# Attention layer on one core: contexts stored unfinished, a third transpose bank, and the mask penalty split between GpSimd and TensorE

## The reference

```python
scale, shift = split(silu(sin_emb(timestep)) @ W_ada + b_ada)
x = ln(src) * (1 + scale) + shift
q, k, v = heads(x @ Wq + bq), heads(x @ Wk + bk), heads(x @ Wv + bv)
scores = q / sqrt(32) @ k.T + attention_bias          # bias: (2, 16, 2048, 2048), 512 MB
scores = where(src_mask, -inf, scores)                # mask: (2, 1, 2048, 2048)
ctx = softmax(scores) @ v
x = x + ctx @ Wo + bo
x = x + gelu2(ln(x) * g2 + beta2) @ W1 ... @ W2 + b2  # gelu2(z) = z * sigmoid(1.702 z)
out = rotate pairs of x by theta and phi
```

## Time and profile before

| | us |
|---|---|
| median of the runs shown | 3857.47 |
| the profiled execution | 3858.61 |
| its span, first to last instruction | 3857.0 |
| phase B, first add to last add and its step | 2172.4 |
| start of phase C, up to its first up-projection | 55.0 |
| the rest of phase C | 1080.6 |

### The profile page before, as it was taken

How to read it: one execution, slowest core, us unless ns; L and a number is a source line. 1 busy time by engine, 2 the same in 40 slices (tenths; PEclk the granted TensorE clock), 3 DMA queues, 4 the chain that set the end, 5 groups by cost and what they waited for, 6 DMA issues and landing times. The chain is left out here.

```text
span 3857.0 us, 64984 instructions
## 1 busy us (share of the span) xinstructions
PE 3589.8 (93%) x18848; PEld 2074.9 (54%) x18848; DVE 2561.2 (66%) x4882; ACT 1899.6 (49%) x2483; POOL 2165.7 (56%) x595
## 2 busy tenths in 40 slices
PE   6778769999999999999999999999699999999997
PEld 2334336666666666666666666666344444444443
DVE  3444449999989999899999899999322323232232
ACT  1221227777777777777777777777211111111110
POOL 0000059999989999999999999999000000000000
PEclk8889879999999999999999999999799999999999
DMA  5556489999999999999999999997511101101000
GB/s 188 169 173 201 147 288 319 315 313 312 319 348 317 316 312 312 337 331 313 317 315 313 341 319 314 317 313 271 155 22 33 22 11 33 22 22 22 11 11 11
DMA packets 327444, 822.20 MB, mean 213 GB/s; under 512 B 165376, under 2 KB 181760, under 8 KB 250624
## 3 DMA queue, kind: packets, MB, share of 16 engines
q1 hardware_dynamic: 277376, 746.44, 57.6%
q10 hardware_dynamic: 45312, 58.74, 5.6%
q0 software_dynamic: 4736, 16.78, 1.2%
HBM read 737.95 MB, written 83.89 MB: 213 GB/s over the span
## 5 line engine op out<-in xcount | busy, mean ns | idle before, releaser
L450 POOL TENSOR_TENSOR ring<-ring,penb 128x2048 f32<-128x2048 f32 x512 | 2089.4, 4119 | 599.6 <-DMA penb<-pen_scratch 542.5
L555 ACT ACTIVATE ring<-ring,neg_max 128x2048 f32<-128x2048 f32 x512 | 1029.1, 2010 | 515.4 <-DVE neg_max L520 515.4
L618 PEld LDWEIGHTS b_T<-ident,ring 128*128 128x128 f32 x8192 | 886.7, 141 | 623.5 <-ACT probT L564 427.6
L618 PE MATMUL b_T<-ident,ring 128*128 128x128 f32 x8192 | 1158.7, 281 | 1.9 <-DVE probT L492 1.3
L492 DVE COPY probT<-b_T 128x512 f32<-128x512 f32 x1024 | 668.0, 684 | 70.5 <-PE b_T L618 70.5
L506 DVE CUSTOM_DVE_ANT_0 ring<-scores,ring,max_part 128x1024 f32<-128x1024 f32 x512 | 657.6, 1284 | 74.2
L506 DVE CUSTOM_DVE_ANT_0 ring<-scores,ring 128x1024 f32<-128x1024 f32 x512 | 622.2, 1215 | 43.6 <-PE scores L601 43.6
L601 PE MATMUL scores<-keys,queries 128*128 (+1 forms) x2048 | 606.5, 418 | 46.6 <-DMA queries<-q_parts 45.4
L781 POOL TENSOR_TENSOR y_out<-rot_a,rot_b 128x512 f32<-128x512 f32 x32 | 50.3, 1572 | 1020.8 <-DVE rot_b L890 1020.0
L564 ACT COPY probT<-b_T 128x512 f32<-128x512 f32 x1024 | 542.8, 580 | 30.2 <-PE b_T L618 24.0
L634 PE MATMUL bank_ctx<-probT,values 128*32 128x512 f32 x4096 | 546.8, 607 | 0.0
(11 more groups left out here) (91 smaller groups left out, 1926.1 us busy)
## 6 DMA issues: line engine op xcount, KB each, us to landing
ring<-in_fside_Bx16xSxS SPq DMA_DIRECT2D x512, 1024.0 KB, 5.8
keys<-k_parts SPq DMA_DIRECT2D x256, 256.0 KB, 6.8
values<-v_heads ACTq DMA_DIRECT2D x128, 256.0 KB, 6.0
queries<-q_parts SPq DMA_DIRECT2D x512, 64.0 KB, 6.8
pen_scratch<-pen SPq DMA_DIRECT2D x8, 2048.0 KB, 7.2
penb<-pen_scratch SPq DMA_DIRECT2D x32, 512.0 KB, 12.3
xin<-in_x ACTq DMA_DIRECT2D x8, 1024.0 KB, 5.2
mask_in<-in_mask_Bx1xSxS_bk ACTq DMA_DIRECT2D x8, 1024.0 KB, 7.3
```

The source lines that it names most:

```text
L450: nc.gpsimd.tensor_tensor(ring[:, j, :], ring[:, j, :], penb[:, j, :], ALU.add).then_inc(masked, 1)
L555: nc.scalar.activation(ring[:, k, :], ring[:, k, :], ACT.Exp, bias=neg_max[:, k:k + 1], accum_out=sums[:, k:k + 1]).then_inc(exp_done, 1)
L618: last = nc.tensor.transpose(bankT[n % 2][:, c * P:(c + 1) * P], ring[:, slot, at:at + P], ident[:])
```

## The change

Phase B:
- GpSimd adds the penalty to columns 0 to 1855 only. For the last 192 columns TensorE adds it, with one more matmul per tile: identity (bf16) times `penb`, accumulated on top of the second half's scores.
- The adds produce the negated sum (`scale=-1`) and its minimum, so that the exponential takes its bias from them directly; `neg_max` is gone. The 8 row minima of a trip are kept in `low_all` by a VectorE copy of 128 x 8 (`keep_low`), once per trip, after the first add of the next trip. The row sums go straight into `sums_all`.
- `close`, the reciprocal and the context product are gone from phase B. `ctxp`, the four partial contexts, is stored as it is: 256 KB instead of 64 KB per unit.
- The bank of `bank_sum` becomes a third transpose bank. Even tiles turn their quarters into banks 0, 1, 2, 0, odd ones into 2, 1, 0, 2.
- VectorE copies quarter 3 of tile i-3 between the two adds of tile i, and quarter 2 of tile i-2 after them.
- TensorE's waits are moved ahead into the group of matmuls before the one that needs them.

Phase C: TensorE transposes reciprocals, widened by VectorE to 128 columns (`recip_wide`), instead of contexts. VectorE adds the four parts (`tensor_reduce`) and multiplies; ScalarE's copy is gone. Contexts are loaded as 4 MB per unit in 16 transfers instead of 1 MB in 4.

The core of the diff:

```diff
-                        nc.gpsimd.tensor_tensor(ring[:, j, :], ring[:, j, :], penb[:, j, :], ALU.add).then_inc(masked, 1)
+                        nc.gpsimd.tensor_tensor(ring[:, j, 0:POOL_MASKED], ring[:, j, 0:POOL_MASKED], penb[:, j, 0:POOL_MASKED], ALU.add).then_inc(masked, 1)
...
+        def turn_bank(t, n):
+            return bankT[(0, 1, 2, 0)[n] if t % 2 == 0 else (2, 1, 0, 2)[n]]
...
-            def copy_quarter(it, j, n):
-                t, k = it * R + j - 2, (j - 2) % R
+            def copy_quarter(it, j, n, lag):
+                t, k = it * R + j - lag, (j - lag) % R
...
+            def keep_low(it, j):
+                if j == 0 and (not known(it) or it > 0):
+                    dve.wait_ge(added, it * R * CH)
+                    nc.vector.tensor_copy(low_all[:, bass.ds(it - 1, 1), :].rearrange("p o n -> p (o n)"), low[:]).then_inc(low_kept, 1)
...
             def step(it, j):
                 add(it, j, 0)
+                keep_low(it, j)
+                copy_quarter(it, j, 3, 3)
                 add(it, j, 1)
-                if live(i, NT):
-                    dve.wait_ge(added, i * CH + CH)
-                    nc.vector.tensor_scalar(neg_max[:, j:j + 1], max_part[:, j, CH - 1:CH], -2.0, 0.5, ALU.mult, ALU.mult).then_inc(max_ready, 1)
-                copy_quarter(it, j, 2)
...
-                copy_quarter(it, j, 3)
...
+                copy_quarter(it, j, 2, 2)
...
             # TensorE, inside score(it, j, c)
+                for n in range(CW // N):
+                    if n == CW // N - 1:
+                        free_before_turn(it, j, c)   # c 0: exp_done t + 1; c 1: out_dve t * 2 - 1
...
+                    if c == CH - 1:
+                        pe.wait_ge(pen_in[j], (it // H) * 16 + 16)
+                        last = nc.tensor.matmul(scores[c][:, CW - PE_MASKED:CW], identb[:], penb[:, j, POOL_MASKED:S],
+                                                start=False, stop=True)
...
             def turn(it, j, n):
                 t, slot = it * R + j - 2, (j - 2) % R
+                for c in range(QR):
+                    if c == 2:
+                        if n == 0 and live(t, NT):
+                            need(pe, out_act, t * 2)
+                        if n == 1:
+                            copied_before_weigh(it, j)
+                        if n == 2 and live(t, NT):
+                            pe.wait_ge(out_act, t * 2 + 1)
...
             def weigh(it, j):
+                for c in range(4):
+                    if c == 2 and live(t, NT):
+                        need(pe, out_dve, t * 2)
+                    if live(unit, UNITS):
                         last = nc.tensor.matmul(bank_ctx[DH * c:DH * (c + 1), :], values[:, hh, QR * n + c, :],
                                                 probT[:, hh, QR * n + c, :], start=(n == 0), stop=(n == 3))
...
-                if j % QT == 2:
-                    close(it, j)
...
             # phase C, VectorE, front(v, f)
                 if f == 0:
+                    nc.vector.tensor_scalar(undefined[:], in_unit(low_all, v), 2.0, 0.0, ALU.mult, ALU.mult)
+                    link(nc.vector.reciprocal(recip[:], in_unit(sums_all, v)), 1)
+                    link(nc.vector.tensor_tensor(recip[:], recip[:], undefined[:], ALU.add), 2)
+                    need(dve, wo_done, v * QT)
+                if f < DB:
+                    need(dve, recip_turned, v * DB + f - 1)
+                    nc.vector.tensor_copy(recip_wide[:, f % 2].rearrange("p t (h d) -> p t h d", d=DH),
+                                          recip[:, 4 * f:4 * f + 4, :].rearrange("p h (t o) -> p t h o", o=1).to_broadcast([P, QT, 4, DH])).then_inc(wide_ready, 1)
+                    dve.wait_ge(part_ld[f % 2], v * 128 + (f // 2) * 64 + 64)
+                    nc.vector.tensor_reduce(ctxT[:, f, :], parts[:, f % 2].rearrange("p g q -> p q g"), AXIS_X, ALU.add).then_inc(parts_used, 1)
+                    dve.wait_ge(parts_used, v * DB + f + 1)
+                    dve.wait_ge(recip_turned, v * DB + f + 1)
+                    nc.vector.tensor_tensor(ctxT[:, f, :], fore[f % 2][:], ctxT[:, f, :], ALU.mult).then_inc(ctxT_ready, 1)
+                if f == 3:
                     dve.wait_ge(xm_ld, v * 16 + 16)
...
             # phase C, TensorE, front(v, f)
                 if f < DB:
-                    if f == 0:
-                        pe.wait_ge(ctx_ld, v * 64 + 64)
+                    pe.wait_ge(wide_ready, v * DB + f + 1)
...
-                        last = nc.tensor.transpose(fore[f % 2][:, t * P:(t + 1) * P], ctx_in[:, t, 4 * f:4 * f + 4, :].rearrange("p h d -> p (h d)"), ident[:])
+                        last = nc.tensor.transpose(fore[f % 2][:, t * P:(t + 1) * P], recip_wide[:, f % 2, t, :], ident[:])
```

More of the change, by code:

```diff
@@ L606, in turn, with free_before_turn @@
+            def free_before_turn(it, j, c):
+                t = it * R + j - 2
+                if live(t, NT):
+                    if c == 0:
+                        pe.wait_ge(exp_done, t + 1)
+                    else:
+                        need(pe, out_dve, t * 2 - 1)
             def turn(it, j, n):
                 t, slot = it * R + j - 2, (j - 2) % R
-                if live(t, NT):
-                    if n == 0:
-                        pe.wait_ge(exp_done, t + 1)
-                    if n < 2:
-                        need(pe, out_dve, t * 2 - 1 + n)
-                    else:
-                        pe.wait_ge(out_act, t * 2 - 1 + n)
-                    for c in range(QR):
-                        at = (QR * n + c) * P
-                        last = nc.tensor.transpose(bankT[n % 2][:, c * P:(c + 1) * P], ring[:, slot, at:at + P], ident[:])
-                    last.then_inc(turned, 1)
@@ L621, in weigh @@
-            def weigh(it, j):
-                n = (j - 2) % QT
-                unit = it * 2 - 2 if j < 2 else it * 2 - 1 if j < 6 else it * 2
-                hh = 1 if 2 <= j < 6 else 0
-                if live(unit, UNITS):
-                    if n == 0:
-                        pe.wait_ge(v_in[hh], it * 16 if j == 2 else it * 16 + 16)
-                        need(pe, ctx_copied, unit)
-                    pe.wait_ge(out_act if n < 2 else out_dve, (unit * QT + QT - 1) * 2 + n % 2 + 1)
-                    for c in range(4):
+                for c in range(QR):
[6 more added lines that the diff above has]
+                            pe.wait_ge(out_act, t * 2 + 1)
+                    if live(t, NT):
+                        at = (QR * n + c) * P
+                        last = nc.tensor.transpose(turn_bank(slot, n)[:, c * P:(c + 1) * P], ring[:, slot, at:at + P], ident[:])
@@ L634, in weigh @@
                         last = nc.tensor.matmul(bank_ctx[DH * c:DH * (c + 1), :], values[:, hh, QR * n + c, :],
                                                 probT[:, hh, QR * n + c, :], start=(n == 0), stop=(n == 3))
-                    if n == 3:
-                        last.then_inc(pv_done, 1)
-            def close(it, j):
-                unit = closing(it, j)
-                if live(unit, UNITS):
-                    pe.wait_ge(ctx_copied, unit + 1)
-                    pe.wait_ge(ctx_normed, unit + 1)
-                    for t in range(QT):
-                        last = nc.tensor.matmul(bank_sum[:, t * DH:(t + 1) * DH], ctxp[:, t * P:(t + 1) * P], sel4[:],
-                                                start=True, stop=True)
-                    last.then_inc(ctx_summed, 1)
+                if live(unit, UNITS) and n == 3:
+                    last.then_inc(pv_done, 1)
@@ L680, in phase_c @@
         sines = sb("sines", [P, B, 2])
[L681 removed]
+        parts = sb("parts", [P, 2, 4, TOK])
+        undefined = sb("undefined", [P, H, QT])
+        recip = sb("recip", [P, H, QT])
+        recip_wide = sb("recip_wide", [P, 2, QT, P])
         xm_in = sb("xm_in", [P, QT, D])
```

200 lines of the change are left out of this document (99 added, 101 removed).

## The result

The changed kernel takes 4294.02 us in the median of four runs (4279.74 to 4311.46), the kernel before 3857.91 beside it: a ratio of 1.113 (1.109 to 1.117). The profiled execution has a span of 4278.1 us against 3857.0, 421.1 more. By the first and last add of half 0 and the end of the span in the two traces: phase A 0.2, phase B 343.1 (first to last of these adds 2511.4 in place of 2168.3), the rest 77.7. 4192 us had been forecast, with a range of 4050 to 4430.

The account below looks back on a forecast made before the run. VectorE was taken to set phase B's pace at 4.20 us a step. 3858.6 + 262 (longer steps) + 10 (`keep_low`) + 63 (phase C), less 1, made 4193, or 4192 us on the median's scale; range 4050 to 4430.

Parts of the forecast that it names:

- The ring: Phase B: scores, add, quarter 3 copy, second half of `weigh`, transposes wait on each other within a step; 4.71 us, +262.
- The held copy: Rival, phase B: `keep_low` waits behind a GpSimd add, 64 x 2.5 = +160 us, 4350 us (4250 to 4430); chance 0.29.
- The likeliest case: Phase B's steps at 4.71 us with `keep_low` unheld, 10 us in all; 4050 to 4290 us; chance 0.48.
- the rival: Phase B: `keep_low` stands behind GpSimd's add in each trip, 2.5 us each, +160 us, 4350 us; chance 0.29.
- the free copy: Phase B: `keep_low` takes 0.15 us per trip, +10 us in all, if nothing holds it; chance 0.48.
- Phase C: Final phase: TensorE's transposes wait for `recip_wide` and VectorE adds parts at the start; +63 us (40 to 80).
- The six boundaries: Phase C, between units: transposes wait for `recip_wide` after the rotation of the unit before; 8.3 us each, +50.
- The first unit: Phase C: no rotation before it, but the same chain through `gate`, `hidden` and the wide copy; +7 us.
- The start: Phase C's very start: VectorE adds four parts four times, 14 us in all; W_o's matmuls begin some 6 us later.
- The engines alone: Phase B: GpSimd, VectorE, TensorE each by itself would allow 3.75 to 3.9 us per step in place of 4.20.
- The cheap ring: Rival, phase B: the late half of `weigh` costs half, a step takes 4.22 us; about 3940 us; chance 0.07.
- The kernel without a ring: Rival, phase B: quarter 3's copy is there in time, TensorE's 3.9 us per step decides; 3777 us; chance 0.16.

Follow-up runs that it names:

- both cuts of the ring: Changed kernel with TensorE's wait for quarter 3's copy moved behind `weigh` (4170.97 us), or with that copy put ahead of its step's first add (4134.19 us).
- low_reduce: Changed kernel with the 128 x 8 minima kept by a VectorE `tensor_reduce` instead of a copy: 4158.24 us, 1.077 of the kernel before.
- late_reduce: Changed kernel with TensorE's wait for quarter 3's copy moved behind `weigh` and the minima kept by `tensor_reduce`: 4034.37 us, 1.048 of the kernel before.

## Why the prediction was right, and where it was off

*The ring, the main step:* right in place and size. Forecast 4.71 us a step, measured 4.67; TensorE stands 0.8 us at the third `weigh` matmul as said; both cuts of the ring brought the step to 3.93 and about it, TensorE's own 3.9, as expected where the ring lets go. Its share of the loss was forecast as 262 us; it is 219, the 343 of phase B less the 124 of the copy below (low_reduce, which has the ring and no held copy, gives 64 x (37.56 - 33.95) = 231). The difference is half 0.04 us a step (20 us), half that the trip before was put at 33.6 us by four steps when its mean, with the slower first trips of each group, is 33.95 (22 us).

*The held copy:* this is the term that was mis-sized. The likeliest case had 10 us for it, the rival 160; low_reduce measured 136. The row that spoke for it, 1.77 in place of 0.34 us up to the end of a GpSimd add, pointed the right way (it is a `tensor_scalar`, not the copy that the prediction calls it, and it began 0.35 us before that add), and the one reason against (only 8 columns) was none: a copy of 8 columns and a `tensor_scalar` of 4 stood as long as what was left of GpSimd's add, and only the `tensor_scalar` of one column never did. Wrong was also that the copy comes at the same place of GpSimd's add in every trip: it began 0.38 to 3.48 us into it, since many of GpSimd's adds start when their slot lands (294 waits for that from 600 to 3000 us). The forecast of 0.48 for the free copy and 0.29 for the held one had the weights the wrong way round. Against the sum of 4193 us the profiled execution took 4279.7: 114 more for the copy (124 in place of 10), 43 less for the ring, 15 more for phase C, 1 for the end of phase B. The likeliest case alone ended at 4290; the total lies in the range because the range took in the held copy, and the ring's 43 us offset part of it. In the sum of the rival the mean duration was put at 2.5 us; it was 1.73, because GpSimd is idle a quarter of the time, but in 14 of 63 trips the clock fell behind it and added 1.5 us: 124 us over the 63 steps against 160. The Trainium skill (SBUF — State Buffer, Who interferes with whom) has it that copies and `tensor_scalar` that use both port pairs exclude a GpSimd instruction for its whole length, that a two-input `tensor_tensor` from SBUF contends with its reads, and that a `tensor_reduce` never does on this chip; the durations above (3.35, 3.70, 3.70 and 0.157 us at most) agree with each.

*Phase C:* +63 forecast, 77.7 measured. The six boundaries were right: 8.2 us each against 8.3. The first unit cost 9.7 against 7. The start was the poor one: from the last add of half 0 to the first up-projection 18.6 us more than before, against 6. VectorE comes to it at 3083.44, once the vectors have landed, and then does four chains in a row:

```profile
3083.44 0.18 DVE L931 TENSOR_SCALAR b_scaled<-b_col 128x16 f32<-128x16 f32 x1 [18.97 <-DMA b_col<-in_L_cond_b]
...
3085.15 3.63 DVE L857 TENSOR_REDUCE ctxT<-parts 128x512 f32<-128x2048 f32 x1
```

A reduce of 2048 elements takes 3.63 us where 2.4 had been estimated from the add of 1024, and the chain of 14 us was counted as partly hidden under the loads, though it begins only after the vectors have landed. It took 21 us, with 1.5 us of waiting for parts in it: W_o's matmuls began 3.5 us after this first row before, and 21.7 us after it here.

*The engines alone:* GpSimd's add 3.74 us (3.75 forecast), 9.4 us of idle time per trip (7 or more), DVE's share 80% (towards 80%), the added matmul 0.1 us of a step. The cheap ring and the kernel without a ring did not come. The latter's 3777 us was too low as well: late_reduce is that kernel (4034 us), and its loads of queries came late.

## What to carry to other kernels

Write down, for each wait that an edit adds, which step's work sets the semaphore's value, and follow the instructions between: a count that is reached inside the same step closes a ring, whose length is the step, whatever the engines' shares say. Look at small VectorE instructions between SBUF tiles beside a busy GpSimd before the large ones, and give them a form that isn't held. When steps get shorter, transfers issued a fixed number of steps ahead are issued fewer microseconds ahead, and the first symptom is one long step per trip, not a full DMA engine.

## What the runs showed of the hardware

- A VectorE copy of 128 x 8 that starts during a GpSimd add of 3.74 us ends 0.03 us after it, in 55 cases of 55 in the changed kernel; a `tensor_scalar` and a two-input `tensor_tensor` of 128 x 4 reached 3.70 us. `tensor_reduce` of the same 128 x 8, `reciprocal` of 128 x 4 (0.17) and `tensor_scalar` of 128 x 1 (0.14) were never held: of 64, 128 and 512 cases 60, 65 and 261 began during such an add.
- Speeding other engines up can make it worse: the copy averaged 1.73 us in a trip of 39.3 and 2.83 in one of 37.6, as its start drew near to that of GpSimd's add.
- One group of small loads issued 4 us earlier raised the DMA engines from 317 to 334 GB/s, with a share of 96% shown before it; at a share of 1.02 in both, 334 GB/s were moved over 2000 us and 345 over 446 us of one execution.
